# Two buffers in place of four for an expert stage's gathers and scatters

## The chip, the cores and the metric

One core of one Trainium2 chip. The metric is the device time of one execution in microseconds (us). TensorE, VectorE, ScalarE, GpSimd and the sync engine (SP) each run their own instruction stream and meet at semaphores; DMA transfers run beside them.

## The reference

The input is 8 x 1024 tokens of width 256, float32. It is normalized, and two branches work on the result: attention with 4 heads, in which the softmax is over the heads of a token, and a mixture of 8 experts of which each token uses two.

```python
xn = layernorm(x)
s = attn(xn, phase, Wq, bq, Wk, bk, Wv, bv, Wo, bo)
# experts, E = 8, FF = 512, K = 2
gates = sinkhorn((xn @ router_w.T + router_b) / temp)      # 3 iterations
topk_vals, topk_idx = top_k(gates, 2)
g = relu(einsum('btd,edf->btef', xn, wg))
p = einsum('btd,edf->btef', xn, wp)
all_out = einsum('btef,efd->bted', g * p, wo)
expert_out = sum of the two chosen rows of all_out, weighted by their gates
out = x + s * silu(xn + expert_out)
```

## The kernel before

The 8192 tokens are treated in 16 blocks of 512. There are three large stages after the set-up: attention of blocks 0 to 3 (`segment(0, QE)`), the expert stage, and attention of blocks 4 to 15 with the joining of both branches (`segment(QE, NQ)`). Every engine has the same order of stages, written out by hand.

The expert stage works on NM = 135 tiles of 128 slots, sorted by expert: two slots for each token and padding. The indices of a tile's tokens come from earlier work and lie in `gidx` (row of `xn_d` to read) and `toks` (row of `y_d` to write). For each tile m:

- GpSimd gathers 128 rows of 1 KB from `xn_d` into a buffer `XG` (L644, an indirect DMA, semaphore `s_g`).
- TensorE turns the tile in two transposes (`gt`, L1127). ScalarE copies the result as the high part (L849), VectorE makes the low part (`xgl`).
- TensorE does the up projection, 12 matmuls (`up`, L1145); ScalarE and VectorE apply the relu and the product (L856, L1656).
- TensorE turns that in four transposes (`ht`, L1154) and does the down projection, 12 matmuls (`down`, L1164).
- ScalarE copies the output into a buffer `YS` (`ye`, L868); GpSimd scatters it to 128 rows of `y_d` (L649, an indirect DMA, semaphore `s_y`).

On TensorE the work of neighbouring tiles is interleaved: iteration m of its loop holds `gt(m+1)`, `up(m)`, `ht(m-1)`, `down(m-2)`. ScalarE's loop has the same shape, with `ye(m-2)` at the end of iteration m. GpSimd's loop issues gather m and then scatter m-7. Gather m waits until the transposes of tile m-4 have read the buffer (`s_gt`), scatter n until `ye(n)` is done (`s_ye`), and `ye(n)` until scatter n-4 has landed, because it writes the same buffer.

An expert's weights (3 MB) are loaded by SP from `w_d` into one of three places in `WR` (`load_expert`, L501). Expert 0 is loaded before the stage, expert 1 once the load before has landed and the first up projection is done, expert 2 after the load before it, and expert x from 3 on once the last tile of expert x-3 is through its down projection. After the last such point SP reloads the matrix M in four pieces (L530), which the later attention blocks use, and then waits for all scatters.

The lines of the loop on GpSimd and of TensorE's loop:

```python
            for m in range(NM + 7):
...
                    if m >= 4:
                        e.wait_ge(s_gt, m - 3)
...
                n = m - 7
                if n >= 0:
                    e.wait_ge(s_ye, n + 1)
```

Of the kernel before, what the change touches and what calls it, by code (L numbers as in the profile page):

```python
# [10 lines left out]
ACT = mybir.ActivationFunctionType  # L11
AX = mybir.AxisListType

NB, S, D, H = 8, 1024, 256, 4
# [4 lines left out]
NM = 2 * NT + E - 1  # L19
# [17 lines left out]
def program(nc, x, phase, Wq, bq, Wk, bk, Wv, bv, Wo, bo, rw, rb, temp, wg, wp, wo, out):  # L37
    ctx = ExitStack()

    def sb(name, shape, dt=F32):  # L40
        return ctx.enter_context(nc.sbuf_tensor(name, shape, dt))

    def sem(name):
        return ctx.enter_context(nc.semaphore(name))

    with ctx:
# [3 lines left out]
        xn_d = nc.dram_tensor("xn_d", [N, D], F32).ap()  # L50
        s_d = nc.dram_tensor("s_d", [N, D], F32).ap()
        u_d = nc.dram_tensor("u_d", [N, H * D], F32).ap()
        y_d = nc.dram_tensor("y_d", [2 * N + NM * 128, D], F32).ap()
# [14 lines left out]
        AUX = sb("AUX", [128, 8192])  # L68
# [24 lines left out]
        with nc.sbuf_tensor("ABR", [128, 2, 512], F32R) as ABR:  # L93
# [4 lines left out]
        AH = sb("AH", [128, 16])  # L98
        RO = AUX[:, 4496:5008].rearrange("p (a d) -> p a d", a=2)
        RO4 = AUX[:, 0:1024].rearrange("p (a d) -> p a d", d=D)  # L100
        XG = [AUX[:, c:c + D] for c in (0, 256, 5120, 5376)]
        XGH = FR[:, 512:1024].rearrange("p (a k n) -> p a k n", a=2, k=2)
        XGL = FR[:, 3584:4096].rearrange("p (a k n) -> p a k n", a=2, k=2)
        ewl = AUX[:, 3350:3350 + NM].bitcast(I32)
# [5 lines left out]
        part = ((AUX[:, 6144:6656], ABR[:, :, :]),  # L110
                (US[:, 0, 0:2, :].rearrange("p c d -> p (c d)"), USR[:, 512:1536].rearrange("p (z f) -> p z f", z=2)),
                (US[:, 1, 2:4, :].rearrange("p c d -> p (c d)"), USR[:, 2048:3072].rearrange("p (z f) -> p z f", z=2)))
        YS = [AUX[:, c:c + D] for c in (2560, 2816, 7168, 7424)]
        toks = AUX[:, 3072:3072 + NM].bitcast(I32)
        gidx = AUX[:, 3072 + NM:3072 + 2 * NM].bitcast(I32)
        rank1h = OH[:, 0:2048].rearrange("p (j r) -> p j r", r=128)
# [6 lines left out]
        ident = sb("ident", [128, 128])  # L123
# [63 lines left out]
        def pM(n):  # L187
# [4 lines left out]
        mG, mP, mX, mH, mY = ps[0:2], ps[2:4], ps[4], ps[5], ps[6:8]  # L192
# [26 lines left out]
        s_uw = [sem(f"s_uw{i}") for i in range(3)]  # L219
        s_us = [sem(f"s_us{i}") for i in range(3)]  # L220
        s_rs = [sem("s_rs0"), sem("s_rs1")]
        s_g = [sem(f"s_g{i}") for i in range(4)]
        s_gt, s_gtc, s_u, s_gr, s_h, s_ht, s_htc, s_dn, s_ye = (
            sem(n) for n in ("s_gt", "s_gtc", "s_u", "s_gr", "s_h", "s_ht", "s_htc", "s_dn", "s_ye"))
        s_y = [sem(f"s_y{i}") for i in range(4)]
        s_cl, s_ct, s_cg = (sem(n) for n in ("s_cl", "s_ct", "s_cg"))
        s_e1, s_et, s_eg, s_e2, s_eo, s_es = (sem(n) for n in ("s_e1", "s_et", "s_eg", "s_e2", "s_eo", "s_es"))
        s_wsp, s_md, s_xtj, s_gi = (sem(n) for n in ("s_wsp", "s_md", "s_xtj", "s_gi"))
# [99 lines left out]
        def _(e):  # L328
# [89 lines left out]
            def load_c(q):  # L418

                y1, y2, xn, xx = cs(q)  # L420
                sl = s_cl if q < NQ - 1 else s_c15
                e.dma_start(y1, blk(y_d, q)).then_inc(sl, 16)
                e.dma_start(y2, blk(y_d[N:2 * N, :], q)).then_inc(sl, 16)
                e.dma_start(xn, blk(xn_d, q)).then_inc(sl, 16)
                if QE < q < NQ - 1:
                    e.wait_ge(s_o, 64 * (q - QE))
                for h in range(H):
                    e.dma_start(xx[h:128:4], rows(xf, q)[h]).then_inc(sl, 16)
# [101 lines left out]
                e.dma_start(M_s[:, :, cols], m_d.rearrange("p (k n) -> p k n", k=2)[:, :, cols]).then_inc(s_ml[j], 16)  # L530
            for i in range(2):
                e.wait_ge(s_rs[i], 16 * 2 * (QE - 1))
            for i in range(4):
                e.wait_ge(s_y[i], 16 * ((NM - i + 3) // 4))
            load_c(QE)
            segment(QE, NQ)
            store_c(NQ - 2)
# [7 lines left out]
        def _(e):  # L545
# [91 lines left out]
            e.wait_ge(s_gi, 1)  # L637
            for q in range(NQ):
                e.wait_ge(s_x[q], 48)
            for m in range(NM + 7):  # L640
                if m < NM:
                    if m >= 4:
                        e.wait_ge(s_gt, m - 3)
                    e.indirect_dma_start(XG[m % 4], None, xn_d,  # L644
                                         bass.IndirectOffsetOnAxis(gidx[:, m:m + 1], 0)).then_inc(s_g[m % 4], 16)
                n = m - 7
                if n >= 0:
                    e.wait_ge(s_ye, n + 1)
                    e.indirect_dma_start(y_d, bass.IndirectOffsetOnAxis(toks[:, n:n + 1], 0),  # L649
                                         YS[n % 4], None).then_inc(s_y[n % 4], 16)  # L650

            def total(q):
                if q < QE:
# [17 lines left out]
            def result(n):  # L671
                r, i = ro(n), n % 4
                _, y2, _, xx = cs(n // 4)
                e.wait_ge(s_pm, n + 1)
                e.wait_ge(s_cg, n // 4 - QE + 1)
                ch(e.tensor_tensor(r, r, y2[:, i, :], ALU.mult))
                e.tensor_tensor(xx[:, i, :], r, xx[:, i, :], ALU.add).then_inc(s_ro, 1)
# [5 lines left out]
            def ahead():  # L683

                _, y2, xn, xx = cs(NQ - 1)
                e.wait_ge(s_cg, NQ - QE)
                for i in range(4):
                    ch(e.tensor_tensor(xn[:, i, :], y2[:, i, :], bo_b[:, :], ALU.mult))
                    e.tensor_tensor(xx[:, i, :], xn[:, i, :], xx[:, i, :], ALU.add).then_inc(s_z, 1)
# [18 lines left out]
        def _(e):  # L708
# [76 lines left out]
            for j in range(18):  # L785
                e.wait_ge(s_m, j + 1)
                if j < 16:
                    k, g, jp = j // 8, j // 2 % 4, j % 2
# [8 lines left out]
            def silu(q):  # L797
                if q < QE:
                    e.wait_ge(s_et, q + 1)
                    e.activation(cE2, cE1, ACT.Silu).then_inc(s_eg, 1)  # L800
                else:
                    e.wait_ge(s_ct, q - QE + 1)
                    y1, y2, _, _ = cs(q)
                    e.activation(y2, y1, ACT.Silu).then_inc(s_cg, 1)
# [58 lines left out]

            def ye(m):
                e.wait_ge(s_dn, m + 1)
                if m >= 4:
                    e.wait_ge(s_y[m % 4], 16 * (m // 4))
                e.activation(YS[m % 4], mY[m % 2][:, 0:256], ACT.Copy).then_inc(s_ye, 1)  # L868

            gt(0)  # L870
            for m in range(NM + 2):
                if m + 1 < NM:
                    gt(m + 1)
                if m < NM:
                    relu(m)
                if 1 <= m <= NM:
                    ht(m - 1)
                if m >= NM:
                    xt(QE, m - NM)
                if m >= 2:  # L880
                    ye(m - 2)
# [4 lines left out]
        def _(e):  # L886
# [3 lines left out]
            for k in range(2):  # L890
                mm = e.transpose(bP[:, 32 + 8 * k:40 + 8 * k], rwN[:, 128 * k:128 * k + 128], ident[0:8, 0:8])
# [96 lines left out]
            for j in range(18):  # L988
# [4 lines left out]
                for c in range(2):  # L993
                    if j < 16:
                        k, g = j // 8, j // 2 % 4
                        mm = e.matmul(mb[j % 5][:, :], WvT[:, 2 * g + c, 128 * k:128 * k + 128], wo_r[:, c, :, :],  # L996
                                      start=(c == 0), stop=(c == 1))
                    else:
                        mm = e.matmul(mb[j % 5][0:4, :], bvT[:, c:8:2], wo_r[:, c, :, :],
                                      start=(c == 0), stop=(c == 1))  # L1000
# [119 lines left out]
            off = {}  # L1120

            def gt(m):
                e.wait_ge(s_g[m % 4], 16 * (m // 4 + 1))
                if m >= 1:
                    e.wait_ge(s_xgl, m)
                for k in range(2):
                    mm = e.transpose(mX[:, 128 * k:128 * k + 128], XG[m % 4][:, 128 * k:128 * k + 128], ident[:, :])  # L1127
                mm.then_inc(s_gt, 1)

            regs = [e.alloc_register(f"eo{i}") for i in range(4)]  # L1130
# [39 lines left out]
            e.wait_ge(s_pm, 4 * QE - 4)  # L1170
            e.wait_ge(s_sm1, 4 * QE - 1)
            gt(0)
            weigh()
            e.wait_ge(s_sm1, 4 * QE)
            e.wait_ge(s_gp, 2)
            e.wait_ge(s_ca, 24 * QE)
            for m in range(NM + 2):
                if m + 1 < NM:
                    gt(m + 1)
                if m < NM:  # L1180
                    up(m)
                if 1 <= m <= NM:
                    ht(m - 1)
                if m >= NM:
                    xt(QE, m - NM)
                if m >= 2:
                    down(m - 2)
# [6 lines left out]
        def _(e):  # L1194
# [329 lines left out]
            def mixed(n):  # L1524
                e.wait_ge(s_mx, n + 1)
                if 2 <= n < 4 * QE - 4:
                    e.wait_ge(s_rs[n % 2], 16 * (n // 2))
                if 4 * QE <= n < 4 * QE + 4:
                    e.wait_ge(s_rs[n % 2], 16 * (n // 2 - 1))
                if n >= 4 * QE + 4:  # L1530
                    e.wait_ge(s_ro, n - 4 * QE - 3)
                if n < 4 * NQ - 4:
                    e.tensor_tensor(ro(n), pM(n), bo_b[:, :], ALU.add).then_inc(s_pm, 1)
                    return
                i = n % 4
                _, y2, _, xx = ends
                e.wait_ge(s_z, i + 1)
                e.tensor_tensor(ro(n), pM(n), y2[:, i, :], ALU.mult).then_inc(s_pm, 1)
                e.wait_ge(s_pm, n + 1)
                e.tensor_tensor(xx[:, i, :], ro(n), xx[:, i, :], ALU.add).then_inc(s_rl, 1)  # L1540
# [144 lines left out]
```

## Time and profile before

| | us |
|---|---|
| median of 3 runs | 1593.45 |
| lowest and highest | 1592.94, 1593.78 |
| the profiled execution, its time | 1593.78 |
| its span, from the first instruction to the last | 1592.0 |
| TensorE busy | 1532.2 |
| VectorE, GpSimd, ScalarE busy | 975.6, 795.5, 730.2 |

The profile is of one execution. An instruction's "idle before" is the idle time of its engine ahead of it, with the releaser named; "DMA to landing" is the time from the start of an issuing instruction to the last semaphore update of its transfer, for those transfers for which the trace shows it. L644 is line 644 of the kernel. PE is TensorE's matmul row, SPq the sync engine's queue of DMA issues. A granted clock of 1.00 is TensorE's full clock.

### The profile page before, as it was taken

What the parts mean: (1) busy time and instruction counts of PE and PEld (TensorE: products, weight loads), DVE (VectorE), ACT (ScalarE), POOL (GpSimd) and SP (SyncE); (2) the same over time, 40 slices, a digit from 0 to 9 for tenths busy, and PEclk for the clock granted to TensorE, in tenths of its full rate; (3) what the DMA queues carried; (4) which work ended last, traced back from release to release, by engine and by line L of the source; (5) the groups of instructions that cost most, each with busy time, mean ns of one, the idle gap of its engine ahead of it and who ended that gap; (6) DMA issues with size and microseconds to landing.
All of it is one profiled execution on the core that took longest, in us unless ns stands there. A gap on an engine that the chain in (4) does not pass through costs nothing.

```text
span 1592.0 us, 32705 instructions
## 1 busy us (share of the span) xinstructions
PE 1532.2 (96%) x11408; PEld 1166.9 (73%) x11408; DVE 975.6 (61%) x1880; ACT 730.2 (46%) x1205; POOL 795.5 (50%) x945
## 2 busy tenths in 40 slices
PE   5999699989999999999999999999999999999997
PEld 2446566668888888888888888776666776666774
DVE  7567989953333333333333333677889788888777
ACT  4766334413333333333333333546456565555552
POOL 4638589913443344334443343253584564853456
PEclk9999899989999999999999999999999999999998
DMA  9989852264233131323111231245555666455464
GB/s 327 395 307 316 300 199 74 78 222 191 64 126 127 63 133 57 124 67 133 55 57 57 81 133 47 93 160 184 172 189 172 206 192 229 143 166 169 151 206 146
DMA packets 162678, 251.22 MB, mean 158 GB/s; under 512 B 13928, under 2 KB 121248, under 8 KB 161376
## 3 DMA queue, kind: packets, MB, share of 16 engines
q1 hardware_dynamic: 147904, 211.47, 38.4%
q0 software_dynamic: 12960, 35.41, 6.7%
q8 instruction: 104, 1.70, 0.4%
q10 hardware_dynamic: 1664, 2.26, 0.4%
q14 instruction: 46, 0.38, 0.1%
HBM read 149.58 MB, written 99.50 MB: 156 GB/s over the span
## 4 chain that ended last, share of the span: by engine, by line
PE 89%; DVE 6%; DMA 2%; ACT 1%; issue 1%; SPq 0%; ACTq 0%; DVEq 0%
PE ps L1145 24%; PE ps L1080 21%; PE ps L1091 13%; PE ps L1164 12%; PE ps L1027 7%; PE ps L1154 4%; PE ps L1048 2%; PE ps L1127 2%; PE ps L996 2%; PE ps L924 1%; DMA WR<-w_d 1%; PE ps L914 1%; PE ps L980 1%; DVE UN L1230 1%; DVE WM L1596 1%
## 5 line engine op out<-in xcount | busy, mean ns | idle before, releaser
L1145 PE MATMUL ps<-WR,FR 128*128 x1620 | 407.6, 400 | 0.7 <-DMA WR<-w_d 0.7
L1145 PEld LDWEIGHTS ps<-WR,FR 128*128 128x128 f32 x1620 | 295.8, 189 | 58.5 <-issue 1.1
L649 POOL DMA_INDIRECT y_d<-AUX x135 | 133.3, 987 | 353.0 <-ACT AUX L868 353.0
L1656 DVE TENSOR_TENSOR AUX<-AUX,ps 128x512 f32<-128x512 f32 x135 | 92.9, 688 | 339.4 <-ACT AUX L856 339.4
L817 ACT ACTIVATE WM<-ps,bcs,trig 128x512 f32<-128x512 f32 x256 | 253.1, 1017 | 86.7 <-PE ps L1080 79.3
L1596 DVE TENSOR_SCALAR WM<-ps,vec,trig 128x512 f32<-128x512 f32 x256 | 244.1, 993 | 61.1 <-ACT WM L817 60.2
L1091 PE MATMUL ps<-WM,XTJ 128*128 128x512 f32 x512 | 237.1, 600 | 0.0
L856 ACT ACTIVATE AUX<-ps 128x512 f32<-128x512 f32 x135 | 80.9, 599 | 315.8 <-PE ps L1145 315.8
L1080 PE MATMUL ps<-XH,WH 128*128 128x512 f32 x512 | 204.7, 400 | 6.1 <-issue 3.8
L1164 PE MATMUL ps<-WR,ABR 128*128 x1080 | 209.4, 292 | 0.0
L1080 PE MATMUL ps<-XH,WL 128*128 128x512 f32 x512 | 199.6, 390 | 0.0
L1080 PE MATMUL ps<-XL,WH 128*128 128x512 f32 x512 | 199.5, 390 | 0.0
L644 POOL DMA_INDIRECT AUX<-xn_d,AUX x135 | 131.6, 975 | 73.8 <-issue 40.1
L1164 PEld LDWEIGHTS ps<-WR,ABR 128*128 128x128 f32 x1080 | 165.4, 190 | 0.0
L1091 PEld LDWEIGHTS ps<-WM,XTJ 128*128 128x128 f32 x512 | 91.6, 190 | 96.6 <-issue 93.5
L661 POOL TENSOR_TENSOR AUX<-AUX,GP 128x256 f32<-128x256 f32 x128 | 81.2, 669 | 149.8 <-DMA AUX<-in_L_attn_x_dram 145.0
L1164 PE MATMUL ps<-WR,FR 128*128 x540 | 152.0, 281 | 0.0
L1027 PE MATMUL ps<-WM 128*64 128x64 f32 x4096 | 131.3, 228 | 16.8 <-DVE TM L1484 14.9
L1027 PEld LDWEIGHTS ps<-WM 128*64 128x64 f32 x4096 | 127.4, 143 | 25.9 <-DVE TM L1484 15.5
L824 ACT ACTIVATE UN<-ps 128x512 f32<-128x512 f32 x128 | 76.2, 596 | 138.8 <-PE ps L1091 135.6
L1080 PEld LDWEIGHTS ps<-XH,WH 128*128 128x128 f32 x512 | 96.3, 188 | 27.4 <-issue 5.2
L1080 PEld LDWEIGHTS ps<-XH,WL 128*128 128x128 f32 x512 | 96.1, 188 | 20.6
(238 smaller groups left out, 2204.1 us busy)
## 6 DMA issues: line engine op xcount, KB each, us to landing
US<-u_d SPq DMA_DIRECT2D x63, 512.0 KB, 5.4
u_d<-UN SPq DMA_DIRECT2D x120, 256.0 KB, 2.0
WR<-w_d SPq DMA_DIRECT2D x8, 3072.0 KB
AUX<-y_d SPq DMA_DIRECT2D x32, 512.0 KB, 5.5
WM<-in_L_attn_x_dram SPq DMA_DIRECT2D x16, 512.0 KB, 9.6
xn_d<-WM SPq DMA_DIRECT2D x32, 256.0 KB, 7.2
w_d<-USR SPq DMA_DIRECT2D x16, 512.0 KB, 5.0
AUX<-xn_d SPq DMA_DIRECT2D x16, 512.0 KB, 6.3
```

The lines of the kernel that those rows point to most:

```text
L644: e.indirect_dma_start(XG[m % 4], None, xn_d, bass.IndirectOffsetOnAxis(gidx[:, m:m + 1], 0)).then_inc(s_g[m % 4], 16)
L649: e.indirect_dma_start(y_d, bass.IndirectOffsetOnAxis(toks[:, n:n + 1], 0), YS[n % 4], None).then_inc(s_y[n % 4], 16)
L661: ins = e.tensor_tensor(y[:, i, :], y[:, i, :], GP[:, i, k, q, None].broadcast_to([128, D]), ALU.mult)
L817: e.activation(rotated(2 * x, i), b, ACT.Identity, bias=bcs[:, x, 0, i:i + 1], scale=trig[:, 0, i:i + 1]).then_inc(s_ca, 1)
L856: e.activation(GR[:, :], mG[m % 2][:, :], ACT.Relu).then_inc(s_gr, 1)
L1027: mm = e.matmul(pS[n % 2][row:row + 64, 64 * c:64 * c + 64].rearrange("p (g t) -> p g t", g=H), QT[:, x, h, col:col + 64], QT[:, 2 + x, h, ...
L1080: mm = e.matmul(b[:, :], w[:, k, 128 * c:128 * c + 128], xx[:, k, :], start=(k == 0 and w is WH and xx is XH), stop=(k == 1 and w is WL))
L1091: mm = e.matmul(b[:, :], XTJ[:, k, a // 2, :], M_s[:, k, 512 * a:512 * a + 512], start=(k == 0), stop=(k == 1))
L1145: mm = e.matmul(b[:, :], x, WR[:, bass.ds(off[m] + (2048 * z + 1024 * a + 512 * k), 512)], start=(k == 0 and x is xh and z == 0), stop=(k ...
L1164: mm = e.matmul(mY[m % 2][:, 0:256], x, WR[:, bass.ds(off[m] + (4096 + 1024 * z + 256 * c), 256)], start=(c == 0 and x is hh and z == 0), ...
L1596: e.tensor_scalar(rotated(2 * x + 1, i), ps[bank(24 * q + c)][:, :], bqk[:, x, i:i + 1], trig[:, 1, i:i + 1], ALU.add, ALU.mult).then_inc( ...
L1656: e.tensor_tensor(HS[:, m % 2, :], GR[:, :], mP[m % 2][:, :], ALU.mult).then_inc(s_h, 1)
```

## The change

The rings of the gathered tiles (`XG`) and of the output tiles (`YS`) go from four buffers to two, with two semaphores each. Gather m waits for the transposes of tile m-2, and the copy `ye(n)` for scatter n-2. In GpSimd's loop the scatter behind gather m is that of tile m-5 in place of m-7.

```diff
--- before.py
+++ after.py
@@ -98,7 +98,7 @@
         AH = sb("AH", [128, 16])
         RO = AUX[:, 4496:5008].rearrange("p (a d) -> p a d", a=2)
         RO4 = AUX[:, 0:1024].rearrange("p (a d) -> p a d", d=D)
-        XG = [AUX[:, c:c + D] for c in (0, 256, 5120, 5376)]
+        XG = AUX[:, 0:512].rearrange("p (a d) -> p a d", a=2)
         XGH = FR[:, 512:1024].rearrange("p (a k n) -> p a k n", a=2, k=2)
         XGL = FR[:, 3584:4096].rearrange("p (a k n) -> p a k n", a=2, k=2)
         ewl = AUX[:, 3350:3350 + NM].bitcast(I32)
@@ -110,7 +110,7 @@
         part = ((AUX[:, 6144:6656], ABR[:, :, :]),
                 (US[:, 0, 0:2, :].rearrange("p c d -> p (c d)"), USR[:, 512:1536].rearrange("p (z f) -> p z f", z=2)),
                 (US[:, 1, 2:4, :].rearrange("p c d -> p (c d)"), USR[:, 2048:3072].rearrange("p (z f) -> p z f", z=2)))
-        YS = [AUX[:, c:c + D] for c in (2560, 2816, 7168, 7424)]
+        YS = AUX[:, 2560:3072].rearrange("p (a d) -> p a d", a=2)
         toks = AUX[:, 3072:3072 + NM].bitcast(I32)
         gidx = AUX[:, 3072 + NM:3072 + 2 * NM].bitcast(I32)
         rank1h = OH[:, 0:2048].rearrange("p (j r) -> p j r", r=128)
@@ -219,10 +219,10 @@
         s_uw = [sem(f"s_uw{i}") for i in range(3)]
         s_us = [sem(f"s_us{i}") for i in range(3)]
         s_rs = [sem("s_rs0"), sem("s_rs1")]
-        s_g = [sem(f"s_g{i}") for i in range(4)]
+        s_g = [sem("s_g0"), sem("s_g1")]
         s_gt, s_gtc, s_u, s_gr, s_h, s_ht, s_htc, s_dn, s_ye = (
             sem(n) for n in ("s_gt", "s_gtc", "s_u", "s_gr", "s_h", "s_ht", "s_htc", "s_dn", "s_ye"))
-        s_y = [sem(f"s_y{i}") for i in range(4)]
+        s_y = [sem("s_y0"), sem("s_y1")]
         s_cl, s_ct, s_cg = (sem(n) for n in ("s_cl", "s_ct", "s_cg"))
         s_e1, s_et, s_eg, s_e2, s_eo, s_es = (sem(n) for n in ("s_e1", "s_et", "s_eg", "s_e2", "s_eo", "s_es"))
         s_wsp, s_md, s_xtj, s_gi = (sem(n) for n in ("s_wsp", "s_md", "s_xtj", "s_gi"))
@@ -530,8 +530,7 @@
                 e.dma_start(M_s[:, :, cols], m_d.rearrange("p (k n) -> p k n", k=2)[:, :, cols]).then_inc(s_ml[j], 16)
             for i in range(2):
                 e.wait_ge(s_rs[i], 16 * 2 * (QE - 1))
-            for i in range(4):
-                e.wait_ge(s_y[i], 16 * ((NM - i + 3) // 4))
+                e.wait_ge(s_y[i], 16 * ((NM - i + 1) // 2))
             load_c(QE)
             segment(QE, NQ)
             store_c(NQ - 2)
@@ -637,17 +636,16 @@
             e.wait_ge(s_gi, 1)
             for q in range(NQ):
                 e.wait_ge(s_x[q], 48)
-            for m in range(NM + 7):
+            for m in range(NM + 5):
                 if m < NM:
-                    if m >= 4:
-                        e.wait_ge(s_gt, m - 3)
-                    e.indirect_dma_start(XG[m % 4], None, xn_d,
-                                         bass.IndirectOffsetOnAxis(gidx[:, m:m + 1], 0)).then_inc(s_g[m % 4], 16)
-                n = m - 7
-                if n >= 0:
-                    e.wait_ge(s_ye, n + 1)
-                    e.indirect_dma_start(y_d, bass.IndirectOffsetOnAxis(toks[:, n:n + 1], 0),
-                                         YS[n % 4], None).then_inc(s_y[n % 4], 16)
+                    if m >= 2:
+                        e.wait_ge(s_gt, m - 1)
+                    e.indirect_dma_start(XG[:, m % 2, :], None, xn_d,
+                                         bass.IndirectOffsetOnAxis(gidx[:, m:m + 1], 0)).then_inc(s_g[m % 2], 16)
+                if m >= 5:
+                    e.wait_ge(s_ye, m - 4)
+                    e.indirect_dma_start(y_d, bass.IndirectOffsetOnAxis(toks[:, m - 5:m - 4], 0),
+                                         YS[:, (m - 5) % 2, :], None).then_inc(s_y[(m - 5) % 2], 16)
 
             def total(q):
                 if q < QE:
@@ -863,9 +861,9 @@
 
             def ye(m):
                 e.wait_ge(s_dn, m + 1)
-                if m >= 4:
-                    e.wait_ge(s_y[m % 4], 16 * (m // 4))
-                e.activation(YS[m % 4], mY[m % 2][:, 0:256], ACT.Copy).then_inc(s_ye, 1)
+                if m >= 2:
+                    e.wait_ge(s_y[m % 2], 16 * (m // 2))
+                e.activation(YS[:, m % 2, :], mY[m % 2][:, 0:256], ACT.Copy).then_inc(s_ye, 1)
 
             gt(0)
             for m in range(NM + 2):
@@ -1120,11 +1118,11 @@
             off = {}
 
             def gt(m):
-                e.wait_ge(s_g[m % 4], 16 * (m // 4 + 1))
+                e.wait_ge(s_g[m % 2], 16 * (m // 2 + 1))
                 if m >= 1:
                     e.wait_ge(s_xgl, m)
                 for k in range(2):
-                    mm = e.transpose(mX[:, 128 * k:128 * k + 128], XG[m % 4][:, 128 * k:128 * k + 128], ident[:, :])
+                    mm = e.transpose(mX[:, 128 * k:128 * k + 128], XG[:, m % 2, 128 * k:128 * k + 128], ident[:, :])
                 mm.then_inc(s_gt, 1)
 
             regs = [e.alloc_register(f"eo{i}") for i in range(4)]
```

## Rows read from the trace of the kernel before

**Rows 1.** The page: busy time of the engines, and the chain that ended last.
```profile
PE 1532.2 (96%) x11408; PEld 1166.9 (73%) x11408; DVE 975.6 (61%) x1880; ACT 730.2 (46%) x1205; POOL 795.5 (50%) x945
...
PE 89%; DVE 6%; DMA 2%; ACT 1%; issue 1%; SPq 0%; ACTq 0%; DVEq 0%
```

**Rows 2.** Windows: length, busy of each engine (instructions), granted clock, DMA share, GB/s.
```profile
343.57:1005.14 661.57, 660.06 (x4080) 584.48 (x4081) 233.36 (x416) 236.42 (x541) 258.51 (x265) 0.99 0.27 95
435.58:445.58 10.00, 10.00 (x64) 8.85 (x63) 3.49 (x7) 3.80 (x10) 3.92 (x4) 1.00 0.89 349
348.00:355.00 7.00, 6.33 (x18) 4.68 (x19) 0.42 (x1) 0.69 (x2) 0.94 (x1) 0.54 0.07 22
1000.00:1003.00 3.00, 2.76 (x25) 2.58 (x24) 1.29 (x2) 1.74 (x4) 0.70 (x1) 1.00 0.00 0
```

**Rows 3.** The timeline of a steady tile: start, us, engine, line, what, [idle before].
```profile
604.79 0.38 PE L1127 MATMUL ps<-ident,AUX 128*128 128x128 f32 x2
...
604.99 0.39 ACT L868 ACTIVATE AUX<-ps 128x256 f32<-128x256 f32 x1 [0.77 <-PE ps L1164]
...
605.65 0.99 POOL L649 DMA_INDIRECT y_d<-AUX  x1 [2.58 <-ACT AUX L868]
...
606.94 0.97 POOL L644 DMA_INDIRECT AUX<-xn_d,AUX  x1 [0.30 <-issue]
...
609.63 0.38 PE L1127 MATMUL ps<-ident,AUX 128*128 128x128 f32 x2
```

**Rows 4.** The gathers (L644): who waited, landings. Then the scatters' (L649) landings.
```profile
  PE ps L1127: 0.8, 1
...
DMA to landing us min/median/max: 2.7/2.8/11.3
...
DMA to landing us min/median/max: 2.4/2.5/8.9
```

**Rows 5.** The waits of the sync engine's queue, 330 to 1010 us.
```profile
SPq L501 <- PE ps L1164: 322.7, 5, 71.4
...
SPq L517 <- DMA WR<-w_d: 52.5, 5, 11.5
```

**Rows 6.** The timeline around the load of expert 3.
```profile
435.58 0.32 SPq L501 DMA_DIRECT2D WR<-w_d  x1
...
436.25 0.99 POOL L649 DMA_INDIRECT y_d<-AUX  x1 [2.57 <-ACT AUX L868]
...
437.55 0.97 POOL L644 DMA_INDIRECT AUX<-xn_d,AUX  x1 [0.31 <-issue]
```

**Rows 7.** Landings: the scatter of 586.3, the gathers of 369.8 and of 911.9.
```profile
DMA to landing us min/median/max: 8.5/8.5/8.5
...
DMA to landing us min/median/max: 8.7/8.7/8.7
...
DMA to landing us min/median/max: 6.6/6.6/6.6
```

**Rows 8.** The timeline of the start of the stage.
```profile
334.74 1.38 POOL L644 DMA_INDIRECT AUX<-xn_d,AUX  x1 [18.21 <-DVE AUX L1576]
...
343.57 0.41 PE L1127 MATMUL ps<-ident,AUX 128*128 128x128 f32 x2 [0.84 <-DMA AUX<-xn_d,AUX]
...
349.25 5.40 PE L1145 MATMUL ps<-WR,FR 128*128 x12 [0.67 <-DMA WR<-w_d]
...
354.63 3.02 PE L1145 MATMUL ps<-WR,FR 128*128 x12
...
355.15 0.94 POOL L644 DMA_INDIRECT AUX<-xn_d,AUX  x1 [5.34 <-PE ps L1127]
...
358.58 0.94 POOL L644 DMA_INDIRECT AUX<-xn_d,AUX  x1 [2.49 <-PE ps L1127]
...
362.80 0.38 PE L1127 MATMUL ps<-ident,AUX 128*128 128x128 f32 x2
```

**Rows 9.** The loads of experts 1 and 2 (L501), first and last start.
```profile
L501 SPq DMA_DIRECT2D WR<-w_d x2: 319/320/320, 354.8 to 366.6; - x2
```

## The prediction, made before the changed kernel was run

> **What bounds the kernel now.** I read the page first, for the engine that fills the span: TensorE is busy for 1532.2 of 1592.0 us and carries 89% of the chain that ended last [rows 1]. The change touches only the expert stage, so I cut that stage out next. From the first gathered tile (343.57 us) to 1005.14 TensorE is busy 660.06 of 661.57 us, while ScalarE, VectorE and GpSimd work 35 to 39% of it [rows 2]. So a delay of anything but TensorE is free until TensorE has to wait, and any idle of TensorE inside the stage is added to the end: no later stage hands time back to an engine that is busy in 96% of the whole span.
>
> Then the timeline of steady tiles [rows 3]. The transposes of a gathered tile (L1127) start at 604.79 and 609.63: a period of 4.84 us. Within it GpSimd issues one scatter (605.65) and 1.29 us after it one gather (606.94), and the scatter waits for ScalarE's copy of an output tile (L868, 604.99). In the whole stage TensorE's waits for a gather sum up to 0.8 us, once [rows 4]. So at depth four nothing shows of a gather's latency, and the question is what two periods less of lead uncover.
>
> **What stays.** The same 135 gathers and 135 scatters are issued by the same engine in the same alternation, on the same queue, and nothing is computed differently. The sync engine waits for two scatter semaphores in place of four at the end of the stage, after 135 scatters either way. I cost that at nothing: behind it stand only loads for a later block.
>
> **The gathers.** Call the tile whose transposes start at 604.79 tile t. Before, gather t+4 runs behind scatter t-4 (the pair at 605.65 and 606.94) and is used four periods after 604.79. Now that slot, behind the same scatter, holds gather t+2. Its new wait, for the transposes of tile t (a buffer is free once they are done), ends at 604.79 + 0.38 = 605.17, before GpSimd is free at 606.94: 1.77 us to spare. So gathers go out at the same moments as now, and what is queued behind that wait, the next scatter, would wait until 610.49 anyway. The lead from issue to use falls from 604.79 + 4 x 4.84 - 606.94 = 17.21 us to 604.79 + 2 x 4.84 - 606.94 = **7.53 us**.
>
> The median gather lands 2.8 us after issue [rows 4], 4.7 us inside that lead. The maximum of that row is 11.3 us, and that decides. Where do the slow ones fall? The sync engine moves an expert's weights (3 MB) with L501, eight times, and after them M in four pieces. The loads of experts 3 to 7 are each released by the end of a tile's down projection (five waits of SP for L1164 [rows 5]), so each starts at the same phase of a period: the one at 435.58 is 0.67 us ahead of a scatter and 1.97 us ahead of a gather [rows 6]. SP waits 10.5 us for such a load to land (52.5 us in 5 waits [rows 5]). A scatter issued 0.7 us after such a start landed after 8.5 us, a gather under expert 2's load after 8.7 us, one under the reload of M after 6.6 us [rows 7]. The first gather of all, under expert 0's load, was issued at 334.74 and released the transposes at 343.57, 8.83 us later [rows 8].
>
> For the gather behind such a scatter no landing is shown at experts 3 to 7. Lower bound: it is in the same queue 1.29 us behind a scatter that takes 8.5, so if both land together it takes 7.2 us, 0.3 inside the lead, and costs nothing. Upper bound: the 11.3 us of rows 4, a stall of 3.8. By bytes: in the 10 us from 435.58 on, 10 x 349 = 3490 KB moved [rows 2], which is the load's 3146 KB and 344 more, room for the scatter (131), this gather (131) and a part of the next scatter; it would land near 445.6, 8.0 us after issue. I take 8.6 us, between the scatter's 8.5 and the other gather's 8.7. **Stall: 8.6 - 7.53 = 1.07 us for each of five loads, 5.4 us**, all on TensorE: its next instructions are these transposes, and the up projection stands behind them. After each, the next gather has the stall added to its lead and meets only the load's tail, so it is in time. The reload of M costs nothing: 6.6 us against 7.53.
>
> Row and rule differ here. The row gives 8.5 us to a 128 KB indirect transfer beside a load, three times its undisturbed time. The Trainium skill, "DMA: Bandwidth & Descriptors", section "Queues, rings and completion order", says that each DMA engine takes its queues in turn, a packet at a time. A gather would then share the engines with the load and be done soon after its undisturbed time, and the sum would be 0 in place of 5.4. The trace does not agree with that, and I go by the row.
>
> **The start of the stage.** Two gathers go out ahead where four did. Gather 2 moves behind the transposes of 343.57, gather 3 behind the next ones, and both are used only after the first up projection (from 349.25, 5.40 us long [rows 8]): leads of some 9 us with no load running for most of them. Gather 4 moves to 355.15, just behind the issue of expert 1's load at 354.8 [rows 9], and is used at 362.80 [rows 8]: a lead of 7.65 us against 8.6, **a stall of 0.95 us**. Gather 5 (358.58 [rows 8]) has until 362.80 + 4.84 = 367.64, 9.1 us. Gather 7 is in the slot of the one that took 8.7 us under load 2, with 7.53 and gather 4's 0.95 of lead: 0.2 at most.
> A possible gain: the first up projection waits 0.67 us for expert 0's weights [rows 8], and 2 x 131 KB fewer move beside that load; at the 349 GB/s of a load in rows 2 that is 0.7 us. I take none of it, since TensorE's clock is at half around there (0.54 from 348 to 355 [rows 2]) and a start inside a half-clock stretch gains little.
>
> **The scatters.** ScalarE's copy of output tile n now waits for scatter n-2. The scatter of 605.65 must have landed by 604.99 + 9.68 = 614.67: 9.02 us, against 2.5 median, 8.5 under loads and 8.9 at most [rows 4, 7]. No wait, by 0.1 to 0.5 us. If one came, the copy of the next gathered tile is queued behind it on ScalarE, whose result the up projection needs only one period later; an engine with 236 of 661 us of work [rows 2] catches up within it. Cost: nothing.
>
> **The sum.** 5.4 + 0.95 = 6.3 us. Against the profiled execution: span 1592.0 + 6.3, plus the 1.8 us outside the span, is 1600.1 us; that execution, at 1593.78, is 0.33 over the median of the three. So 1593.45 + 6.3 = **1599.8 us**, 0.4% slower.
>
> **The rivals.**
> *Hidden anyway* (1593.5, up to 1596.6 with stalls of half the size). For it: the lower bound of 7.2 us, and that a miss of 1.07 us is small against what I don't know of where in the load a gather is served; each stall must exceed 0.5 us for the total to be seen. Against: 8.83 us from issue to use at expert 0 [rows 8]. The rule of queues taken in turn, above, points here. Chance 0.22.
> *The clock falls at each stall.* TensorE ran at half clock around 350, and the first up projection took 5.40 us where the next took 3.02 [rows 8]: 2.4 us. Six such and the 6.3 make 20.7: 1614 us. Against: from 1000 to 1003 TensorE was busy 2.76 of 3.00 us, with breaks around its transposes, and the clock stayed at 1.00 [rows 2]; six stalls of 1.1 us in dense matmuls are not much more. The Trainium skill, "TensorE: Matmul & The Clock Gate", section "HAM oscillation — how this bites in real kernels", tells of a kernel in which a DMA wait in every tile took the clock down each time; here a wait would come in one tile of some twenty. Chance 0.07.
> *The gathers land as late as the 11.3 us row*: 3.8 x 5 + 3.65 = 22.5 us, 1616. That row is from the start, with four gathers in a row and other traffic; against it stand 8.5 and 8.7. Chance 0.05 for over 1608.
> *Faster.* The start decides: with 262 KB less beside expert 0's load the first up projection starts up to 0.67 us sooner, and if that takes it out of the half-clock stretch 2.4 us more are saved: 3.1 us, 1590.4. It decides only where no gather stalls, from landings of 7.5 us down, and is barely to be told even then. Chance 0.03.
>
> **How the numbers follow.** Forecast, stalls of 0.5 to 2.4 us at the loads: 0.63, between 1596.7 and 1608, likeliest 1599.8. Hidden 0.22, clock 0.07, far later landings 0.05, faster 0.03. A measurement of this kernel tells 0.2%, 3.2 us, from no change. Faster 0.03; same 0.22; slower 0.63 + 0.07 + 0.05 = 0.75. Leaving the no-change case out would leave out over 2 in 10, so the range starts below it and ends with the forecast's own: 1593.2 to 1608.
>
> **What would show it.** In the profile after: idle of TensorE ahead of L1127, put down to the gather's DMA, about six times and some 1 us each, near 363 and about two periods after each L501 from the fourth on; no wait of ScalarE's L868 for a scatter; a steady period still of 4.84 us; undisturbed gathers and scatters still at 2.8 and 2.5 us; clock 1.00 after 355. It is wrong if the waits are absent, if there is more than one per load (a late gather passing its delay on), or if the granted clock dips in the stage.

## The result, and the profile after

The changed kernel takes 1612.77 us (median of 4 runs, 1607.59 to 1614.43) against 1593.62 us before in the same session: ratio 1.0109, 95% interval 1.0087 to 1.0132, 19 us slower by these medians, 17 by the ratio. The forecast was 1599.8 us, slower by 6, with a range to 1608: the direction was right, the size was a third of what came. Over all 23 runs of the changed kernel the times lie between 1606 and 1617 us, with a median of 1610.6, and they go with the mean clock granted to TensorE: 0.986 to 0.988 in the runs of 1606 to 1609, 0.981 to 0.985 in those of 1614 to 1617. The kernel before spreads as widely: in the three sessions of the experiments it took 1585 to 1597 us.

The profiled execution of the changed kernel is one of the quickest, span 1604.5 us, 12.5 over before's. Its page, against [rows 1]:

```profile
PE 1536.4 (96%) x11408; PEld 1169.5 (73%) x11408; DVE 974.2 (61%) x1880; ACT 730.0 (45%) x1205; POOL 794.2 (49%) x945
...
PE 88%; DVE 5%; DMA 4%; ACT 1%; issue 1%; POOL 0%; ACTq 0%; SPq 0%; DVEq 0%
```

DMA has gone from 2% to 4% of the chain. Next, who waits on TensorE inside the expert stage, from 355 to 1000 us; the same view of the kernel before has no row at all (columns: total, times, longest):

```profile
PE ps L1125 <- DMA AUX<-xn_d,AUX: 8.1, 6, 2.1
PE ps L1143 <- issue: 3.1, 5, 0.7
PE ps L1143 <- DVE FR L1635: 0.9, 1, 0.9
PE ps L1143 <- DMA WR<-w_d: 0.7, 1, 0.7
```

The first row was forecast: six waits of the transposes for a gather. The other three, 4.7 us ahead of the up projection (L1143 now), were not. In the trace they stand behind each of the six waits, 0.66 us four times, 0.67 and 0.91, and once more, 0.48, where no wait for a gather is seen (at 940.03, beside the reload of M). The windows of the stage, of the stage behind it, and of two pieces in which an up projection follows a late gather:

```profile
342.54:1022.38 679.84, 665.11 (x4095) 586.72 (x4091) 234.79 (x418) 237.80 (x543) 261.34 (x267) 0.99 0.26 93
1022.38:1604.50 582.12, 570.03 (x5144) 394.72 (x5144) 469.30 (x870) 321.47 (x405) 314.25 (x401) 0.99 0.54 176
448.00:451.40 3.40, 3.30 (x17) 2.80 (x18) 0.31 (x1) 0.26 (x1) 0.91 (x1) 1.00 0.26 82
768.00:771.50 3.50, 3.21 (x8) 2.59 (x9) 0.42 (x1) 0.04 (x1) 0.91 (x1) 0.57 0.26 80
```

And those windows before:

```profile
343.57:1006.70 663.13, 661.49 (x4090) 585.72 (x4091) 234.06 (x417) 237.12 (x543) 259.38 (x265) 0.99 0.27 95
1006.70:1592.00 585.30, 572.41 (x5144) 396.34 (x5144) 469.99 (x870) 322.52 (x405) 314.10 (x401) 0.99 0.53 175
```

From the first transposes to the first matmul of the next stage it was 663.13 us and is 679.84, so the stage is 16.7 us longer. This pair of executions hides a part of it: the stage behind took 585.30 before and 582.12 after, and the first transposes start 1.0 us earlier, 16.7 - 3.2 - 1.0 = 12.5. The last two windows of the changed kernel show that late gathers differ in what follows: after one the clock is 1.00, after another 0.57.

One late gather, in the timeline of the changed kernel (start, duration, engine, line), against [rows 3, 6]:

```profile
436.30 0.32 SPq L501 DMA_DIRECT2D WR<-w_d  x1
...
438.26 0.97 POOL L643 DMA_INDIRECT AUX<-xn_d,AUX  x1 [0.30 <-issue]
...
441.09 3.00 PE L1143 MATMUL ps<-WR,FR 128*128 x12
...
447.00 0.44 PE L1125 MATMUL ps<-ident,AUX 128*128 128x128 f32 x2 [1.05 <-DMA AUX<-xn_d,AUX]
...
448.10 3.01 PE L1143 MATMUL ps<-WR,FR 128*128 x12 [0.66 <-issue]
...
452.80 0.38 PE L1125 MATMUL ps<-ident,AUX 128*128 128x128 f32 x2
```

The load goes out at 436.30, the gather 1.96 us behind it, and its transposes start 447.00 - 438.26 = 8.74 us after its issue; 8.6 was forecast. Then 0.66 us pass between the transposes and the up projection, where there is no gap in a steady tile. The source view of the line that loads a register for the up projection (TENSOR_LOAD on TensorE's queue) tells what stands there. Before, at the steady tile of [rows 3], and after, at this one (min/median/max ns, start):

```profile
L1134 PEldq TENSOR_LOAD <-eoff x1: 298/298/298, 602.9 to 602.9; - x1
```
```profile
L1132 PEldq TENSOR_LOAD <-eoff x1: 304/304/304, 447.0 to 447.0; - x1
```

Before, the load runs at 602.9, 1.9 us ahead of the transposes of 604.79, while the array is still busy with matmuls issued earlier. After, the sequencer sits in the wait for the gather, and the load starts only when that ends. There are two of them in a row, 0.30 us each (the second from 447.5), and TensorE idles meanwhile.

### The profile page after: what moved, and what is told of

Its sections match the earlier page's. It is cut to its first block, busy times and chain, and to the rows that moved or that the text cites. A ratio compares the mean times of both kernels' runs of the same rounds, so it can differ in the third digit from the quotient of the medians.

```text
span 1604.5 us, 32706 instructions
## 1 busy us (share of the span) xinstructions
PE 1536.4 (96%) x11408; PEld 1169.5 (73%) x11408; DVE 974.2 (61%) x1880; ACT 730.0 (45%) x1205; POOL 794.2 (49%) x945
## 4 chain that ended last, share of the span: by engine, by line
PE 88%; DVE 5%; DMA 4%; ACT 1%; issue 1%; POOL 0%; ACTq 0%; SPq 0%; DVEq 0%
PE ps L1143 21%; PE ps L1078 21%; PE ps L1089 13%; PE ps L1162 11%; PE ps L1025 7%; PE ps L1152 3%; DMA AUX<-xn_d,AUX 3%; PE ps L1046 2%; PE ps L1125 2%; PE ps L994 2%; PE ps L922 1%; PE ps L978 1%; PE ps L912 1%; DVE UN L1228 1%; DMA WR<-w_d 1%
## 5 line engine op out<-in xcount | busy, mean ns | idle before, releaser
L1143 PE MATMUL ps<-WR,FR 128*128 x1620 | 408.4, 401 | 5.7 <-issue 3.1
L1143 PEld LDWEIGHTS ps<-WR,FR 128*128 128x128 f32 x1620 | 296.6, 190 | 65.0 <-issue 7.6
L1635 DVE TENSOR_TENSOR FR<-ps,FR 128x256 fp32r<-128x256 f32 x135 | 57.3, 425 | 93.2 <-ACT FR L847 93.2
```

The source lines that it names most:

```text
L1143: mm = e.matmul(b[:, :], x, WR[:, bass.ds(off[m] + (2048 * z + 1024 * a + 512 * k), 512)], start=(k == 0 and x is xh and z == 0), stop=(k ...
```

## The experiments

Twelve kernels were run, 5 rounds each, on three chips. The kernel before took 1590.0, 1589.2 and 1590.3 us in the three sessions; each "over before" below is against the runs of its own session. The ratio's interval is 95%.

**Which ring it is.** `e1_gather4_scatter2` and `e2_gather2_scatter4` each do one half of the change. The edits to the kernel before, cut to their core (waits and semaphores follow):

```diff
 # e1_gather4_scatter2
-        YS = [AUX[:, c:c + D] for c in (2560, 2816, 7168, 7424)]
+        YS = [AUX[:, c:c + D] for c in (2560, 2816)]
 # e2_gather2_scatter4
-        XG = [AUX[:, c:c + D] for c in (0, 256, 5120, 5376)]
+        XG = [AUX[:, c:c + D] for c in (0, 256)]
-                n = m - 7
+                n = m - 5
```

> Only the scatter's ring goes to two; the gathers keep four buffers and their lead of 17.2 us. If the loss comes from late gathers alone: 1593.5 +- 1 us, TensorE waits for a gather once (0.8 us, at the start), no wait of L868's copy for a scatter. If the ring of output tiles has a part in it (its cover was only 0.1 to 0.5 us): ScalarE waits for scatters under the loads, and the time is 1597 or more.

> Only the gather's ring goes to two; output tiles keep four. If late gathers are the whole cause: the time of the full change, 1606 to 1616 us from run to run, with six waits of TensorE of 0.9 to 2.1 us. If the output ring carries half of the loss: about 1602.

Measured: e1 1589.92 us, ratio 0.9997 (0.9982 to 1.0012); no wait of ScalarE for a scatter, and none of TensorE from 355 to 990 us. e2 1612.70 us, ratio 1.0141 (1.0111 to 1.0172), with six waits for gathers, 7.3 us in its profile. Within these intervals the gathers' ring is the whole loss.

`e3_gather3_scatter2` has three buffers for gathers (`XG` of three, its waits and the lag of scatters to match).

> Three buffers for gathers, two for outputs: the lead is 7.53 + 4.84 = 12.4 us. If a gather beside a load takes 8.5 to 10 us from issue to use, as in the profile after: no waits beyond the first, the time of before within 1 us. If gathers also slow down because of the shallow ring itself: part of the loss stays.

Measured: 1589.22 us, ratio 1.0002 (0.9988 to 1.0015), no waits of TensorE from 355 to 990. One more buffer is enough.

**Whether it is the loads, and what of them.** `e7_small_load` leaves most of five loads out:

```diff
-                e.dma_start(WR[:, b:b + 6144].bitcast(F32), w_d[128 * x:128 * x + 128, :]).then_inc(s_wl, 16)
+                n = 6144 if x < 3 else 64
+                e.dma_start(WR[:, b:b + n].bitcast(F32), w_d[128 * x:128 * x + 128, 0:n]).then_inc(s_wl, 16)
```

> The changed kernel, in which the loads of experts 3 to 7 move 64 of 6144 columns, so their tiles are computed with old weights; the same instructions otherwise. If the loads make the gathers late: five of six waits go, the one near 363 (expert 1's load) stays, 2 to 4 us over before. If anything else of the expert change (the SP's wait, registers) does: five waits stay and 1606 or more.

Measured: 1594.21 us, ratio 1.0031 (1.0016 to 1.0047), 5 us over before. The tiles of experts 3 to 7 are computed with old weights here, so only the time counts. Five waits are gone, the one beside expert 1's load is left (1.4 us, with 0.7 ahead of the up projection). So the loads make the gathers late. The remainder is larger than I expected, with 0.5 us more beside the reload of M.

`e5_load_in_pieces` moves the same bytes in four transfers (an edit to the changed kernel):

```diff
-                e.dma_start(WR[:, b:b + 6144].bitcast(F32), w_d[128 * x:128 * x + 128, :]).then_inc(s_wl, 16)
+                n = 4 if x else 1
+                for j in range(n):
+                    if j and j == n - 1:
+                        e.wait_ge(s_wq, 48 * x)
+                    w = 6144 // n
+                    e.dma_start(WR[:, b + w * j:b + w * j + w].bitcast(F32),
+                                w_d[128 * x:128 * x + 128, w * j:w * j + w]).then_inc(s_wl if j == n - 1 else s_wq, 16)
```

> The changed kernel, but the loads of experts 1 to 7 go out as four transfers of 768 KB, the fourth once the first three have landed. If a gather is late because a load that is one 3 MB transfer holds each DMA engine until it is through: the gather gets in between pieces and lands in 4 to 7 us (6.4 to 6.6 beside the reload of M, which has four pieces), inside the lead of 7.53; waits gone or nearly, 1593 to 1598 us. If only the bytes count (3 MB ahead or beside, however cut): landings stay at 8.7 and the time at 1606 to 1616.

Measured: 1593.52 us, ratio 1.0019 (1.0004 to 1.0035), 3.5 over before in place of 19. The timeline at expert 3's load:

```profile
437.46 9.44 SPq L506 DMA_DIRECT2D WR<-w_d  x4
...
439.42 0.97 POOL L649 DMA_INDIRECT AUX<-xn_d,AUX  x1 [0.30 <-issue]
...
446.95 0.38 PE L1131 MATMUL ps<-ident,AUX 128*128 128x128 f32 x2
...
447.48 2.81 PE L1149 MATMUL ps<-WR,FR 128*128 x11 [0.15 <-issue]
```

The transposes start 7.53 us after the issue, with no wait for the gather. But there is still a small gap ahead of the up projection: a gather that lands shortly before it is needed holds the sequencer long enough that the register loads are not done in time. In the whole stage these gaps are 1.9 us in 5 places. So the gather gets through sooner, but the edit changes three things at once, and this run doesn't tell them apart. The transfers are shorter. The fourth goes out only at 446.58, once the first three have landed, so that a quarter of the bytes is no longer ahead of the gather. And the packets of a load are smaller, as the view of the DMA queues shows for the changed kernel from 436 to 447 us, then for this one from 437 to 446.5 (packets, MB, share):

```profile
q1 hardware_dynamic: 144, 3.15, 73.5%
```
```profile
q1 hardware_dynamic: 432, 2.36, 70.2%
```

The whole load is 128 packets of 24 KB, a row each, and 16 small ones; the three pieces are 384 of 6 KB and 48 small ones. The reload of M speaks against the bytes alone. It sends 4 MB in four transfers with no wait between them; in the changed kernel the first goes out at 924.84, and the gather of 926.80, again 1.96 us behind it, landed after 5.8 us, the next one after 7.2. (The expectation above says 6.4 to 6.6; these traces show 5.8 to 7.2.)

**What a break of TensorE costs.** `e4_registers_first` is the changed kernel with the two register loads moved ahead of the wait for the next gather:

```diff
             def up(m):
-                e.reg_load(regs[m % 4], eoff[0:1, m:m + 1])
-                off[m] = e.snap(regs[m % 4], min_val=place_e(2), max_val=place_e(0))
-                e.reg_load(wreg[m % 2], ewl[0:1, m:m + 1])
...
             for m in range(NM + 2):
+                if m < NM:
+                    places(m)     # the three lines taken from up(m)
                 if m + 1 < NM:
                     gt(m + 1)
```

> The changed kernel, but TensorE's sequencer loads the two registers of an up projection ahead of its wait for the next gather instead of behind it. If the 0.66 us ahead of the up projection after each late gather are these register loads, no longer run ahead: those gaps go, six of them, -4 us, and with shorter breaks the clock falls less often, so 1600 to 1608 in place of 1606 to 1616. If the gap is VectorE's low part (the chain copy, subtraction, of the same tile) or something else: unchanged, 1606 to 1616.

Measured: 1600.53 us (1597.64 to 1604.28), ratio 1.0067 (1.0050 to 1.0085): 10.5 over before, where e2, with the same gather ring, is 22.7 over. Its timeline at one late gather:

```profile
597.50 0.44 PE L1125 MATMUL ps<-ident,AUX 128*128 128x128 f32 x2 [1.21 <-DMA AUX<-xn_d,AUX]
597.79 3.03 PE L1145 MATMUL ps<-WR,FR 128*128 x12
...
602.53 0.38 PE L1125 MATMUL ps<-ident,AUX 128*128 128x128 f32 x2
```

The wait is there as ever, six of them with 7.4 us in all, and the gap ahead of the up projection is gone. Twelve microseconds are a lot more than 6 x 0.66 = 4. The rest goes with the clock (a mean of 0.985 over the runs of e2, 0.987 over those of e4), which the next three take apart without any late gather.

`e8_plain_stalls` is the kernel before, with TensorE held at six tiles by two additions on GpSimd:

```diff
+        HELD = (22, 37, 53, 69, 85, 100)
 # GpSimd, ahead of scatter n
+                if n + 3 in HELD:
+                    e.wait_ge(s_dn, n + 1)
+                    ch(e.tensor_tensor(TM[:, 0:256], TM[:, 0:256], TM[:, 0:256], ALU.add))
+                    e.tensor_tensor(TM[:, 0:256], TM[:, 0:256], TM[:, 0:256], ALU.add).then_inc(s_jk, 1)
 # TensorE, ahead of gt(m + 1)
+                if m in HELD:
+                    e.wait_ge(s_jk, HELD.index(m) + 1)
```

> The kernel before, with four buffers, in which TensorE is held at six tiles (22, 37, 53, 69, 85, 100) before the next gathered tile's transposes until GpSimd has done two additions of 128x256 (about 0.67 us each) that start when the previous down projection is done. No gather is late. If a break of TensorE costs what it lasts and no more: 6 x 1.4 = 8.4 us over before. If each break also uncovers the register loads (0.66 us) and lets the clock fall in a part of the cases, as late gathers seem to: 6 x 2.06 = 12.4 us directly and 3 to 10 more through the clock, so 15 to 22 over before, with a mean granted clock below before's.

`e9_stalls_registers_first` is that with the edit of e4; `e12_longer_stalls` is e9 with three additions in place of two.

> As e8_plain_stalls, with the register loads ahead of the wait. If register loads and clock make up the excess: 8 to 12 us over before, the step down from e8_plain_stalls being over 4 us, since shorter breaks also spare the clock. If a break costs what it lasts alone: the same as e8_plain_stalls.

> As e9_stalls_registers_first, with three additions on GpSimd in place of two: breaks of about 2.1 us, the wait and register loads of e8_plain_stalls together, but no register load in them. Directly 6 x (1.79 + 0.7) = 15 us over before. If it is the length of the break that lets the clock fall (1.6 us each, three times in the profile of e8_plain_stalls): some 5 us more, 18 to 23 over before and a mean clock near 0.984. If the register loads or the order of the instructions have to do with it: 15 over before, clock at 0.988.

| kernel | median us | over before, us | ratio (interval) | mean clock, this and before |
|---|---|---|---|---|
| e8: 1.44 us wait + registers | 1611.57 | 22.4 | 1.0141 (1.0119 to 1.0163) | 0.9842, 0.9883 |
| e9: 1.44 us wait | 1598.11 | 9.0 | 1.0068 (1.0045 to 1.0091) | 0.9893, 0.9883 |
| e12: 2.13 us wait | 1610.19 | 19.9 | 1.0121 (1.0092 to 1.0151) | 0.9843, 0.9879 |

Two of the six breaks in e8's timeline:

```profile
530.03 0.44 PE L1133 MATMUL ps<-ident,AUX 128*128 128x128 f32 x2 [1.44 <-POOL TM L652]
531.12 2.99 PE L1151 MATMUL ps<-WR,FR 128*128 x12 [0.66 <-issue]
535.82 0.38 PE L1133 MATMUL ps<-ident,AUX 128*128 128x128 f32 x2
...
610.01 0.44 PE L1133 MATMUL ps<-ident,AUX 128*128 128x128 f32 x2 [1.44 <-POOL TM L652]
...
611.11 4.61 PE L1151 MATMUL ps<-WR,FR 128*128 x12 [0.66 <-issue]
...
617.43 0.38 PE L1133 MATMUL ps<-ident,AUX 128*128 128x128 f32 x2
```

and the clock behind each of them (windows, the third column from the right):

```profile
531.00:534.50 3.50, 3.38 (x17) 2.88 (x18) 0.34 (x1) 0.35 (x1) 1.10 (x2) 1.00 0.25 77
611.60:615.00 3.40, 3.40 (x10) 2.63 (x9) 0.00 (x0) 0.00 (x0) 0.78 (x1) 0.51 0.22 77
```

The two breaks are the same to a hundredth, and the second costs 1.6 us more: the up projection takes 4.61 us in place of 2.99, because the clock is at half, 1.2 GHz, for most of it. In this profile three of the six breaks end so. Between the starts of transposes the rows give the price of a break: 617.43 - 610.01 = 7.42 and 535.82 - 530.03 = 5.79, against 4.84 steady; so 0.95 us behind the wait without a fall of the clock, 2.58 with one. In e9 it is 611.64 - 606.61 = 5.03, 0.19:

```profile
600.18 0.38 PE L1133 MATMUL ps<-ident,AUX 128*128 128x128 f32 x2
...
606.61 0.44 PE L1133 MATMUL ps<-ident,AUX 128*128 128x128 f32 x2 [1.44 <-POOL TM L652]
...
611.64 0.38 PE L1133 MATMUL ps<-ident,AUX 128*128 128x128 f32 x2
```

e12 answers what does it, the register loads or the length of the break. It has no register load in its breaks, and the clock falls again, in four of six; one with and one without:

```profile
531.58 0.44 PE L1134 MATMUL ps<-ident,AUX 128*128 128x128 f32 x2 [2.13 <-POOL TM L653]
...
536.61 0.38 PE L1134 MATMUL ps<-ident,AUX 128*128 128x128 f32 x2
...
611.52 0.44 PE L1134 MATMUL ps<-ident,AUX 128*128 128x128 f32 x2 [2.13 <-POOL TM L653]
...
618.12 0.38 PE L1134 MATMUL ps<-ident,AUX 128*128 128x128 f32 x2
```

Breaks of 2.1 us, in one piece or as 1.44 and 0.66 around the transposes, let the clock fall in a part of the cases and cost 20 to 22 us for six; breaks of 1.44 us did not in this profile, and cost 9. Length alone doesn't decide it. In the profile after and in e2's, twelve breaks of 1.55 to 3.01 us (wait and gap together) hold only two falls, behind 1.90 and 2.01 us, and the longest, 2.10 and 0.91, is followed by none.

**Ways out.** `e6_transposes_later` has TensorE do `up(m)` ahead of `gt(m + 1)` in the changed kernel; `e10_pieces_registers` has the edits of e5 and e4 together; `e11_before_registers` has the edit of e4 in the kernel before.

> The changed kernel, but TensorE does the up projection of a tile before the transposes of the next gathered one. They are then used about 3.1 us later in the period, and the new wait of GpSimd ends later too (behind 608.3 in the steady tile in place of 606.9), so the lead becomes about 9.2 us, against 8.6 to 9.8 measured from issue to use. If lateness is all: most waits gone, the rest under 0.6 us, 0 to 4 us over before. If the later copy of the gathered tile then holds up the next up projection in every tile: 0.2 us or more times 135, over 27 us slower than before.

> The changed kernel with the loads in pieces and the register loads ahead of the wait, both. With pieces alone 3.5 us over before were left, of which 0.15 to 0.6 us at each load stood ahead of the up projection. If those are register loads behind a gather that is only just in time: they go, and two buffers run as fast as four, within 1.5 us of before. If the pieces themselves cost: 3 us over before stay.

> The kernel before with the register loads ahead of the wait. With four buffers TensorE's sequencer is ahead anyway, so only the first up projection, 0.67 us, can gain: 0 to 1 us faster than before, and more than 1 us slower only if register loads ahead of the transposes hold those up at the start.

Measured: e6 1595.62 us, ratio 1.0025 (1.0011 to 1.0040), 5 over before, more than the 0 to 4 expected; one wait is left from 355 to 990, 1.1 us beside expert 1's load, and since the profile is of its fastest run (1588.95), what the others lose stays open. e10 1590.13 us, ratio 0.9999 (0.9982 to 1.0016): two buffers are as fast as four. e11 1590.38 us, ratio 0.9996 (0.9980 to 1.0011): no gain to be told. No version beats the kernel before; e10 equals it with half the buffers.

## Why the prediction was right and wrong

*What holds.* The lead of 7.53 us, GpSimd's unchanged rhythm, the places of the stalls (six, at the loads of experts 1 and 3 to 7, none elsewhere), no wait of ScalarE for a scatter: all as forecast. The reload of M makes TensorE wait for no gather either, but it is not free: a gather issued at 931.64 landed after 7.2 us and was used at 939.16, so late that the register loads behind it were uncovered for 0.48 us. The steady period is still 4.84 us, and e1, e2 and e3 show that the gathers' ring is the cause, e7 that the loads are.

*The lateness* was sized at 6.3 us and is 8.1 in the profile after, 7.3 in e2, 7.4 in e4. One gather took 9.8 us from issue to use (issued at 677.30, its transposes at 687.09, after a wait of 2.10) where I had 8.6. The rule on queues taken in turn, which spoke for no stall at all, was read too narrowly: the same section of the Trainium skill, "DMA: Bandwidth & Descriptors", "Queues, rings and completion order", says that an engine drains a whole packet of one queue before it switches. The trace has the sizes: 128 packets of 24 KB in the load, 128 of 1 KB in the gather, as many of one as of the other. As an estimate, a gather whose packets take turns with as many of the load ends about when the load does: 10.5 us after the load's start, 8.5 us after the gather's own issue, against 8.5 to 9.7 measured. Read so, the rule spoke for the stall, and the prediction's sentence that the trace does not agree with it was wrong. It is a fit and no test: M comes in packets of 4 KB (1085 for 4.19 MB), eight times as many as the gather's, so the same estimate gives 1.3 us of turns on top of the undisturbed 2.8, some 4 us, where 5.8 to 7.2 were measured.

*The step that failed* is the price of a stall: "Stall: 8.6 - 7.53 = 1.07 us for each of five loads", with 0.95 us for expert 1's. I took a stall to cost its own length. Six of them were to cost 6.3 us; in the profile after the stage grew by 16.7. A stall costs three things more. First, the register loads behind the wait, which ran ahead under earlier matmuls, are uncovered: 4.7 us in the profile after, 0.66 at most places. I had named what is queued behind GpSimd's new wait and not what is queued behind TensorE's. The rows to see it by were in the trace of before, in TensorE's own queue. Second, a break costs more than the idle time that the view shows: e9's price per break is 1.59 + 0.19 (606.61 - 600.18 = 6.43 us between transposes, 1.59 late), 1.78 for a wait shown as 1.44, so some 0.35 us more each, 2.1 for six. What this part is made of was not taken apart. Third, the clock.

*The clock* was a rival, at 0.07 and 1614 us: all six stalls, 2.4 us each. It is neither that nor nothing. That rival's time is near the measured one by luck, since the time is made up otherwise. Lateness and register loads add up to breaks of some 2 us, near which the clock falls in a part of the cases, 1.6 us each. In the profile after it fell once: 8.1 + 4.7 + 2.1 + 1.6 = 16.5. That this is close to the 16.7 us that the stage grew is partly chance: from the fourth tile on the periods between transposes are 17.4 us over 4.84 each, and the first three are 13.6 us in place of 14.4, which e8 has too (13.7) with four buffers. The 0.9 us that the sum lacks are mostly the register loads, which cost 0.76 a break (0.95 - 0.19) in place of the 0.66 shown. How often the clock falls in the median run is only bounded: 19.2 us over before by the medians of four, less 14.9 for the other three parts, leave 4.3; 17.0 by the median of all 23 runs leave 2.1: one to three falls. I had set against this rival a stretch with the clock at 1.00 in which TensorE was still busy 92% of the time; six breaks of 2 us are not like that, and without the uncovered register loads my own 1.1 us breaks would probably not have let it fall, as in the profiles of e4 and e9 (1.0 to 1.5 us, twelve breaks, no fall). So the second error fed on the first: e9 and e8 differ by 0.66 us a break, and by 13.5 us in the time.

Left open: why single gathers take 9.8 us in place of 8.7, which of the three things that e5 changes lets the gather through, and why of equal breaks some let the clock fall and others don't.

## What to carry to other kernels

A ring's depth is set by the slowest transfer that falls into its lead, not by the median: look for what large transfers run beside it, at what phase they start, and how large their packets are against its own. Price a wait on the engine that sets the end by everything that its queue did ahead of time behind it, register loads above all, then by the part of the break that no idle time shows, then by what the break does to the clock; put cheap sequencer work ahead of a wait that can be late. And where a deep ring is too dear, cut the long transfer beside it into pieces first.

## What the runs showed of the hardware that was not expected

A gather of 128 rows of 1 KB took 2.8 us undisturbed, and 8.5 to 9.7 us to land beside one transfer of 3 MB in 24 KB packets; with that transfer in four pieces, the last held back, it was in time for 7.53, and beside four of 1 MB it took 5.8 to 7.2. Of the breaks of equal length in dense matmuls (2.1 us in all), 3 of 6 in one profile and 4 of 6 in another were followed by a stretch at half clock that cost 1.6 us; of six of 1.44 us, none, and a break of 3.0 us in the changed kernel passed without one. A register load in TensorE's queue takes 0.30 us and was free where the queue was ahead of the array (no gap ahead of the up projection in a steady tile; moving the loads forward in the kernel before, e11, gained nothing).
